# Head softmax on one Trainium2 core: TensorE makes the older tile's products with the values ahead of the coming scores

## What is computed

```python
qkv = x @ w_qkv + b_qkv                       # 16 heads of 8
qkv = qkv.reshape(b, n, 3, N_HEADS, HEAD_DIM)
q, k, v = transposed to (b, head, n, 8)
dp = jnp.einsum('bhqd,bhkd->bhqk', q, k) * SCALE
attn = jax.nn.softmax(dp, axis=1)             # over the 16 heads
w_avg = jnp.einsum('bhqk,bhkd->bhqd', attn, v)
out = w_avg @ w_proj + b_proj                 # added to x
```

## Time and profile before

| | |
|---|---|
| median of three runs | 2295.32 us |
| lowest and highest run | 2286.49 us, 2296.2 us |
| profiled execution | 2285.96 us |
| its span in the profile | 2284.2 us |
| VectorE busy over the span | 1675.7 us (73%) |
| TensorE matmuls busy over the span | 1869.8 us (82%) |
| ScalarE, GpSimd busy over the span | 1107.3 us (48%), 1022.5 us (45%) |
| first and last score matmul of step 6 | 1334.5 us, 1940.1 us |

### The profile page before, as it was taken

How to read it: one execution, slowest core, us unless ns; L and a number is a source line. 1 busy time by engine, 2 the same in 40 slices (tenths; PEclk the granted TensorE clock), 3 DMA queues, 4 the chain that set the end, 5 groups by cost and what they waited for, 6 DMA issues and landing times.

```text
span 2284.2 us, 32109 instructions
## 1 busy us (share of the span) xinstructions
PE 1869.8 (82%) x12288; PEld 1210.5 (53%) x12288; DVE 1675.7 (73%) x2158; ACT 1107.3 (48%) x1830; POOL 1022.5 (45%) x382
## 2 busy tenths in 40 slices
PE   7988999854888885559999977788878777499998
PEld 5444444343444444447777754455555455377776
DVE  4655556255899985547777689999999999467666
ACT  2344445421634322115555566666676766355554
POOL 3476767411277750110000048788888999300000
PEclk8898999876999997669999999899999999699999
DMA  2112111000200000011010000000000000100000
GB/s 70 29 38 48 29 29 29 1 10 11 37 0 0 1 1 10 5 47 42 15 37 19 1 1 1 1 1 1 2 1 2 1 2 1 42 28 28 14 1 19
DMA packets 34014, 37.53 MB, mean 16 GB/s; under 512 B 5763, under 2 KB 21382, under 8 KB 33862
## 3 DMA queue, kind: packets, MB, share of 16 engines
q1 hardware_dynamic: 33334, 34.43, 6.0%
q10 hardware_dynamic: 528, 1.05, 0.2%
HBM read 19.48 MB, written 1.05 MB: 9 GB/s over the span
## 4 chain that ended last, share of the span: by engine, by line
PE 40%; issue 19%; DVE 19%; POOL 14%; ACT 4%; DMA 2%; SPq 1%; POOLq 0%; DVEq 0%; ACTq 0%; PEldq 0%
PE ps L46 9%; PE ps L47 8%; PE ps L48 7%; DVE negm L2122 7%; POOL AF L685 6%; POOL hc L1274 3%; POOL AF L1274 3%; PE ps L489 2%; PE ps L473 2%; PE ps L514 1%; DVE AF L2129 1%; PE ps L853 1%; POOL AR_plain L1982 1%; DVE AR L1063 1%; DVE AR L1057 1%
## 5 line engine op out<-in xcount | busy, mean ns | idle before, releaser
L1083 DVE TENSOR_TENSOR AF<-ps,AF 128x512 f32<-128x512 f32 x256 | 176.9, 691 | 182.8 <-ACT AF L1037 181.9
L2122 DVE TENSOR_REDUCE negm<-ps 128x64 bf16<-128x1024 f32 x256 | 302.4, 1220 | 11.3 <-PE ps L1999 11.2
L685 POOL TENSOR_TENSOR AF<-AF 128x2048 f32<-128x2048 f32 (+3 forms) x73 | 234.2, 3209 | 153.8 <-ACT AF L625 147.8
L46 PE MATMUL ps<-XH,AR 128*128 128x512 f32 x616 | 257.1, 417 | 35.1 <-DVE AF L894 18.1
L1037 ACT ACTIVATE AF<-ps 128x512 f32<-128x512 f32 x256 | 152.9, 597 | 260.6 <-PE ps L48 258.6
L1982 POOL TENSOR_TENSOR AR_plain<-AF 128x2048 f32<-128x2048 f32 x64 | 261.8, 4092 | 38.2 <-ACT AF L2076 37.4
L2096 ACT ACTIVATE AF<-ps 128x1024 f32<-128x1024 f32 x192 | 196.5, 1023 | 146.6 <-PE ps L2008 144.8
L47 PE MATMUL ps<-XL,AR 128*128 128x512 f32 x616 | 248.0, 403 | 0.0
L48 PE MATMUL ps<-XH,AR 128*128 128x512 f32 x616 | 247.3, 402 | 0.0
L2008 PE MATMUL ps<-negm,ident_bf 128*128 128x512 bf16 x512 | 161.0, 397 | 96.3 <-DVE negm L2122 96.1
L625 ACT ACTIVATE AF<-ps 128x512 f32<-128x512 f32 (+1 forms) x304 | 155.6, 576 | 146.0 <-PE ps L476 82.8
(11 more groups left out here) (309 smaller groups left out, 3948.2 us busy)
## 6 DMA issues: line engine op xcount, KB each, us to landing
AR<-AR SPq DMA_DIRECT2D x96, 128.0 KB, 2.4
AF<-in_L_ffn_Wg_dram SPq DMA_DIRECT2D x19, 256.0 KB, 2.7
AF<-in_L_ffn_Wu_dram SPq DMA_DIRECT2D x19, 256.0 KB, 3.0
AF<-in_L_ffn_Wd_dram SPq DMA_DIRECT2D x19, 256.0 KB, 3.8
AF<-AF SPq DMA_DIRECT2D x16, 64.0 KB, 2.4
AF<-AR_plain SPq DMA_DIRECT2D x16, 64.0 KB, 2.4
out_dram<-X SPq DMA_DIRECT2D x1, 1024.0 KB, 5.1
AF<-in_L_attn_a_Wq_dram SPq DMA_DIRECT2D x1, 512.0 KB, 4.0
```

Of the source, the lines that this page charges most:

```text
L46: pe.matmul(out, ah, bh, start=start, stop=False)
L685: pool.tensor_tensor(zacc[u % 2][:, :, c0:512], zacc[u % 2][:, :, c0:512], pt[t % 4][:, :, 0:w], ALU.add).then_inc(s0_zp, 1)
L1083: dve.tensor_tensor(mh[:, m % 3, :], bank(2 + m % 2), msg[:, m % 3, :], ALU.mult).then_inc(m_h, 1)
L2122: dve.tensor_reduce(negm6[:, j % 4, :], bank(2 * (j % 3), 2).rearrange("p (j q i) -> p q j i", j=HJ, i=2), mybir.AxisListType.XY, ALU.max, ...
```

## The change

In the loop over the halves j, the call of `pv` for the tile of four tiles ago moves ahead of the call of `scores(j + 2)`. It stays behind `subtract(j)`. Nothing else is changed, and no instruction is added or removed.

```diff
             for j in range(2 * NTI):
                 subtract(j)
+                if j // 2 >= LAG:
+                    pv(j // 2 - LAG, j % 2)
                 if j + 2 < 2 * NTI:
                     scores(j + 2)
-                if j // 2 >= LAG:
-                    pv(j // 2 - LAG, j % 2)
             for m in range(NTI - LAG, NTI):
                 pv(m, 0)
                 pv(m, 1)
```

## The result

The change made the kernel slower by 1.67% (ratio 1.0167, 95% interval 1.0136 to 1.0198): 2329.66 us median of four runs, against 2291.1 us for before in four runs (three of them gave the 2295.32 us of the table above). The profiled execution took 2324.01 us. Its span is 2322.2 us, 38.0 us more than the 2284.2 of before.

What follows compares the result with a forecast made beforehand. VectorE was taken to set the pace in the head softmax, TensorE mattering only where VectorE waits. Jobs 18.9, group starts 17.1 and projections 2.0 summed to 38.0 us, all in that stage: 2329 us, range 2305 to 2350.

Steps and rivals of the forecast that it cites:

- Ordinary tiles: Tiles without job, group start or projection: scores still ready 1.5 and 1.1 us before VectorE wants them, so no loss.
- The cover of 1.1 us: Ordinary tile, new order: second scores ready 1.1 us before VectorE wants them; before the change 0.57 us more.
- Jobs: Scores behind a job: 12 places at 1.15 us, transposes 0.4, two value jobs 2.7 and 2.0; sum 18.9 us.
- Group starts: First tile of a group: both scores behind products waiting for stack; seven places at 2.3 us, sum with the eighth 17.1.
- The eighth place: Group start at a value job, no VectorE operation in its stack, TensorE idle only 1.1 us; put at 1.0 us.
- Projections: Projection ahead of second scores: 2.8 us in seven later groups, 1.8 behind six late starts, minus 2.6 for additions; 2.0 us.
- the middle of the two bases: Whole kernel: 2324 us from the profiled execution, 2333 from the median of timed runs; the middle, 2329 us, was stated.
- Only the group starts cost: Rival: jobs are hidden because VectorE has more to do after a stack; 19 us, 2305 to 2314 us; chance 0.12.
- TensorE becomes the bound for whole tiles: Rival: after group starts half clock lasts through the projection, 16 us more; 2340 to 2349 us; chance 0.15.
- Nothing changes: Rival: VectorE's order and work stay, scores always have their cover; 2286 to 2295 us; chance 0.05.
- Faster: Rival: VectorE's waits vanish if a group's first product no longer waits for stack; at most minus 14 us; chance 0.03.
- the sum at full clock: Group starts replayed with 0.57, 0.26 and 0.82 us: 1.4 us a place, the sum 6 us less.

Runs made afterwards that it cites:

- the first experiment: Against before: value products ahead of scores only in half tiles without group start, job, transposes or projection (ordinary tiles only); ratio 1.0013.
- jobs only: Against before: value products ahead of scores only in second halves followed by a job or by transposes; ratio 1.0113.
- the early stack: With the change's order on TensorE: VectorE's stack moved ahead by half a tile, to behind the first maxima; ratio to before 1.0010.
- the early stack with the order of before: Against before: VectorE's stack moved ahead by half a tile, TensorE's order not changed; ratio 0.9969.
- with TensorE kept busy: Against the changed kernel: unused extra score matmuls, four times at seven group starts, ahead of the waiting value products; ratio to before 1.0094.
- the kernel with projections ahead: Against before: value products ahead of scores only in second halves followed by a projection (projections only); ratio 1.0067.
- the group starts only: Against before: value products ahead of scores only in the first tile of each group of eight, both halves; ratio 1.0066.
- before with TensorE kept busy: Against before, its order kept: unused extra scores, two more times at seven group starts, ahead of the waiting value products; ratio 0.9981.
- the last with the early stack: Against before: stack half a tile earlier, all value products ahead of scores, projection, jobs and transposes behind them; ratio 0.9961.

## Why the prediction was right, point by point

**What bounds the step.** Right. In the stretches compared VectorE's work did not change by more than 0.2 us, and by its waits (30.6 us in the step before, 68.9 after) 38.3 us are its idleness.

**Ordinary tiles: nothing.** Right by the first experiment. The cover of 1.1 us was read too large, though. TensorE holds 1.69 us per half tile in the new order, not 1.58, as this ordinary tile of the change shows:

```profile
1962.40 0.64 PE L2032 MATMUL ps<-hc,AF 128*8 128x128 f32 x16
...
1962.97 0.74 PE L1999 MATMUL ps<-AF_rounded,AR 128*128 128x256 f32 x4
1963.55 0.60 PE L2008 MATMUL ps<-negm,ident_bf 128*128 128x512 bf16 x2
1964.09 0.64 PE L2032 MATMUL ps<-hc,AF 128*8 128x128 f32 x16
```

From products to products it is 1.69 us, with 0.54 us from the subtraction to the products where I had taken the 0.26 us that it has to the scores in the earlier trace rows.

**Jobs: 18.9 us forecast, 19.9 measured.** Twelve at 1.02 us are 12.2 (13.8 forecast at 1.15). The transposes cost nothing (0.4). The first value job cost 3.96 + 0.44 us (2.7), because the clock fell during it: with jobs only, at full clock, it cost 2.63. Its successor cost 1.76 (2.0). The job of tile 10, forecast as hidden, cost 1.58 us at a fallen clock.

**Group starts: 17.1 us forecast, 13.3 measured.** The seven first waits make 16.5 us and the six second ones 8.5, against 11.0 before: 14.0 (forecast 16.1). The first is the 2.6 us of the replay less 0.3, of which 0.2 is that the scores behind the slow products took 1.22 us and not 1.42. The second maximum came 1.8 us later than before, not 2.3, as the clock was back for the second scores (0.77 us). The eighth place cost nothing, and even lost the 0.75 us that VectorE waited there, where I had put 1.0: that was a guess.

**Projections: 2.0 us forecast, 5.2 measured.** Mis-sized. A later group costs 0.68 us, not 0.4, from the 1.69 us above, and there are eight and not seven. Six behind a late group start cost 2.3 (1.8). The additions gave back 2.6, as forecast.

Together 19.9 + 13.3 + 5.2 = 38.4 us, against 38.0 in the span. The median, 2329.66 us, lies where the middle of the two bases had put it. The forecast of 38.0 was met to this degree by luck: the errors of the terms, +1.0, -3.8 and +3.2, cancel. The mechanism was right at each kind of place, but the honest accuracy is that of the terms: 5% for the jobs, 22% for the group starts, and the projections cost two and a half times what was forecast.

**The rivals.** "Only the group starts cost" fell by the experiment with jobs only. "TensorE becomes the bound for whole tiles" did not come: the clock was back within 5 us of the start of the products. "Nothing changes" fell, as VectorE's waits are made by the order on TensorE. The rule of the Trainium skill, page "Perfetto Trace Analysis", section "Identifying the Most-Contended Engine", names VectorE rightly here (95% busy in the stretch). "Faster" fell. Its point of decision, the wait for the stack, was the right one: with the early stack, which shortens it, the change's order costs 12 us and not 39, and the early stack with the order of before is faster than before.

**The clock.** The Trainium skill, page "TensorE: Matmul & The Clock Gate", section "What's actually happening", was drawn on for which replay to take. The trace agrees that the lower level follows the idle gap (0.56 against 1.00 with TensorE kept busy), though the last section has falls of the clock without a long gap. By the sum at full clock I had said 6 us less; measured are 11.9 us at the seven places, since 2.33 + 1.33 became 1.45 + 0.46. The replay was not wrong in this, but its base was. The 1.4 us a place count from a kernel before that is at full clock too, and before is at 0.50 at that place. Against before as it is, 0.57, 0.82 and 0.26 us in the earlier trace rows put the second maximum at 1482.75 in place of 1482.68, some 0.1 us later and not 1.4; measured are 1.45 + 0.46 = 1.91 us of waits against 1.87.

## What to carry to other kernels

On an engine that works its list in order, what moves ahead of the operation that the bounding engine needs next is not only the moved work but its waits and all that is called behind it; list them, and compare each with the time by which that operation is early. Put work that may wait behind it. And the wait that stalled TensorE for 3 us here was paid twice, once as idleness and once as half clock behind it; moving the operation waited for by half a tile was worth more than any order around the wait.

## What the runs showed of the hardware

The granted clock fell also without a long gap. During the value jobs TensorE is busy with 16 matmuls of 128 columns for some 3 us. In before the granted clock stays at 1.00 there. In the kernel with projections ahead the first value job starts at 1633.04 and the clock fell at 1635.0, in the middle of the same instructions. It was 1.00 ahead of this and still 0.50 from 1637 to 1640 us, with TensorE busy throughout:

```profile
1633.10:1634.60 1.50, 1.50 (x9) 1.22 (x9) 1.50 (x2) 0.00 (x0) 1.50 (x1) 1.00 0.00 0
...
1637.00:1640.00 3.00, 3.00 (x25) 1.85 (x23) 1.67 (x2) 1.65 (x3) 0.53 (x1) 0.50 0.00 0
```

TensorE's last gap ahead of it is 0.75 us, before the job. The same fall, 1.6 to 2.0 us into the first value job, is in three more kernels: the change, the group starts only, and before with TensorE kept busy. In five others (all of the rest but before, ordinary tiles only and the last with the early stack) it came 2.7 to 3.7 us after the start of one of the two value jobs. In three kernels with the job's order of before (projections only, group starts only, before with TensorE kept busy) the maxima wait 4.6 us beside these jobs, against 0.2 in before. What decides is open; it was not tried.

From start to start, TensorE takes 0.54 us from a subtraction to products, 0.57 to scores and 0.58 to the next subtraction in the new order, and 0.26 us to scores, 0.75 to products and 0.57 to the next subtraction in the old. These are 1.69 and 1.58 us, 0.11 us more a half tile for the new order, with the same instructions.

VectorE's L233 takes 0.34 us where GpSimd is idle. Where it starts during GpSimd's product (L1982) it ends with it, as in before:

```profile
1401.91 4.09 POOL L1982 TENSOR_TENSOR hc<-XN,AF 128x2048 f32<-128x2048 f32 x1 [3.44 <-ACT AF L2076]
...
1403.70 2.40 DVE L233 TENSOR_SCALAR R<-X,mv,rstd 128x128 f32<-128x128 f32 x1
```

The product ends at 1406.00 and L233 at 1406.10. With the group starts only one L233 took 4.17 us, beside a product from 1412.42 to 1416.47. No experiment was made on this. Between the profiles of this study it makes up to 5 us of difference (3.0 to 7.7 us for the eight L233 of the step).
